# Two packed attentions of a four-layer model: each round cut into two halves of two heads, with the plain score products issued inside the halves

## The chip, the cores and the metric

The kernel runs on one core of one Trainium2 chip. The time is the device time of the whole kernel in microseconds (us), the median of a few executions; lower is better. Engines are called by their short names: PE is TensorE (matrix products, results in PSUM banks), DVE is VectorE, ACT is ScalarE, POOL is GpSimd, SP issues the loads.

## What is computed

The reference is four layers on `x` (2 batches, 256 tokens, width 128), each an attention (mostly over a context of 512 keys) and a feed-forward part, added to `x`:

```python
x = x + _L1_xattn_ref(_layernorm(x), ctx_1024, ctx_1024, mask_SxS2_bk0, Wq, Wk, Wv, Wo)   # 16 heads of 8, 512 keys, masked
x = x + _L1_ffn_ref(_layernorm(x), ...)   # begins with self-attention: 16 heads of 8, 256 keys; then a mixture of experts
```

The change touches only these two attentions, called L1x and L1f below. Both have 16 heads of width 8: scores = q·k, softmax over the keys, times the values.

## The kernel before

**Packing.** A head of width 8 would use 8 of PE's 128 rows. Four heads (a "head group", `HG = 4`, `NG = 4` groups) are laid on the four quarters of 32 rows: head j of a group on rows 32j to 32j+31. A product on one quarter and products on other quarters can run side by side in PE. Queries and keys are held in three 8-row parts (high and low halves of a 16-bit split), so a quarter has 24 used rows.

**Iterations and rounds.** An iteration `it` is one head group and one batch (8 in all). A round `r` takes 256 keys of an iteration: L1x has 512 keys, so `rpi = 2` rounds per iteration and 16 rounds; L1f has 256 keys, `rpi = 1`, 8 rounds.

**What a round does.** The softmax needs the row maximum before the exponential. The scores are therefore computed twice:

1. `natural(nr, part)` (L676), the plain products: queries on the output's rows, one product of 512 columns per head and query tile (L1x), or two of 256 (L1f). Four of them, numbered `w`, belong to a round, two in each `part`; head quarter j is `w % 4`. They go to a ring of three PSUM banks (S0, S1, M; `ring`, L637), and DVE takes the maximum of each (`stat`, L1830 in L1x with the mask, L1824 in L1f), which empties the bank.
2. `spread(it)` writes the maxima of an iteration into a matrix `m16`, by three small operations: on DVE for the first two iterations (L1836 to L1838), on POOL after that (L2453 or L2456, L2459, L2462).
3. `turn_max(it)` (L691) turns `m16` on PE into a ring bank, and DVE's `with_max` (L1846) adds it to the queries.
4. `scores(r)` (L713): keys on the output's rows, maxima included: 8 products of 256 columns, four heads times two key tiles (`cc`), into two pairs of PSUM banks, one pair for heads 0 and 1, one for heads 2 and 3. Ahead of them, in all 128 rows, four products of 512 columns bring in the mask (L702, L1x) or two are there to keep PE busy (L705, L1f).
5. ACT takes the exponential of each pair of banks (L1409, two per round).
6. `values(r-1)` (L727): 8 products of 32-bit data, each as two instructions, in quarters of columns, into bank O.

Every fourth round (L1x) or second round (L1f) ACT copies bank O out (L1434), PE turns it (`turn_out`, L736) and DVE divides by the sums (`norm`, L1854 to L1857). For the next head group PE repeats the queries (`RQ`, L661), and in L1f the keys (`RK`, L637), in a ring bank, and ACT copies them out.

**Order on PE.** The order is written by hand in `pe_packed`. The plain products run `lead = rpi + 1` rounds ahead. An iteration of the loop is: `scores(r)`, `natural(r+lead, 0)`, `values(r-1)`, `turn_max` when an iteration of heads begins next, `RQ`/`RK`, `turn_out`, `natural(r+lead, 1)`. Where no plain products are left, spare products (L381) stand in their place; some also stand in the head (L684, two after each part).

**Order on DVE.** `stat` 0 and 1, `with_max`, `norm`, `stat` 2 and 3, then `spread` for the first two iterations.

**POOL.** Before it spreads maxima, POOL splits seven blocks of values for layer 2 into halves (`FILL`; L2550 the high half, L2553 the rest). While it waits for maxima later, it splits layer 2's weights and context (L2515, L2517).

Of the kernel before, what the change touches and what calls it, by code (L numbers as in the profile page):

```python
# [25 lines left out]
P = 128  # L26
B, S, D = 2, 256, 128
# [59 lines left out]


# [5 lines left out]
DVE_SPREADS = 2  # L94
L1X = Packed("L1x", SK, mask=True)
# [30 lines left out]
def build(nc, A, out):  # L126
    with ExitStack() as ctx:
# [527 lines left out]
        def pe_packed(pe, a, last_v):  # L655
# [8 lines left out]
            def natural(nr, part):  # L664
# [6 lines left out]
                for w in range(4 * s + 2 * part, 4 * s + 2 * part + 2):  # L671
# [22 lines left out]
            def scores(r):  # L694
                it, c = divmod(r, rpi)
                g, b = divmod(it, B)
                for hp in range(2):
                    if r:
                        pe.wait_ge(sem(f"{n}.exp"), 2 * r - 1 + hp)
                    for hh in range(2 if a.mask else 1):  # L700
                        if a.mask:
                            pe.matmul(pairs[hp][:, hh, :], ident16[:],  # L702
                                      maskT[:, 2 * c:2 * c + 2, :].rearrange("p k q -> p (k q)"), start=True, stop=False)
                        else:
                            pe.matmul(pairs[hp][:, hh, :], ident16[:], ident16[:].unsqueeze(1).broadcast_to([P, 4, P]),  # L705
                                      start=True, stop=True)
# [11 lines left out]
            def values(r):  # L718
                it, c = divmod(r, rpi)
                g, b = divmod(it, B)  # L720
                pe.wait_ge(sem(f"{n}.exp"), 2 * r + 2)
                if g and b == 0 and c == 0:
                    pe.wait_ge(sem(f"{n}.out"), g)
                for cc in range(2):
                    kc = 2 * c + cc
                    for j in range(HG):
                        mm = pe.matmul(bank["O"][HR * j:HR * j + VR, b * S:(b + 1) * S], Vaug[:, b * kt + kc, HG * g + j, :],  # L727
                                       PX[(2 * r + j // 2) % 4][:, j % 2, cc * S:(cc + 1) * S],
                                       start=(kc == 0), stop=(kc == kt - 1))
                mm.then_inc(sem(f"{n}.pv"), 1)  # L730
# [20 lines left out]
            for r in range(-a.lead, a.rounds + 2):  # L751
                if r == 0:
                    for b in ("S3", "T0", "T1", "O"):
                        if fills[b]:
                            pe.wait_ge(free[b], fills[b])
                if 0 <= r < a.rounds:
                    scores(r)
                if r + a.lead < a.rounds:
                    natural(r + a.lead, 0)
                if r == 1:  # L760
                    for v in last_v:
                        emptied(pe, v)
                if r + a.lead >= a.rounds and r <= a.rounds:
                    ring_spare(pe, a, 4 if r == a.rounds else 2)
                if 1 <= r <= a.rounds:
                    values(r - 1)
                if (r + 1) % rpi == 0 and 0 <= (r + 1) // rpi < NG * B:
                    turn_max((r + 1) // rpi)
# [14 lines left out]
                if r + a.lead < a.rounds:  # L783
                    natural(r + a.lead, 1)
# [800 lines left out]
        def _(dve):  # L1585
# [228 lines left out]
            def packed(a, last=(), behind=()):  # L1814
                n, rpi, kt = a.name, a.rpi, a.kt

                def stat(nr, k):
                    it, s = divmod(nr, rpi)
                    w = 4 * s + k
                    ps = filled(dve, f"{n}.N{it}.{w}")  # L1820
                    if w == 0 and it >= DVE_SPREADS + 2:
# [5 lines left out]
                    if nr or k >= 2:  # L1827
# [906 lines left out]
```

## Time and profile before

| | |
|---|---|
| median of 3 runs | 543.66 us (543.61 to 546.74) |
| the profiled execution | 545.07 us in all, span 543.4 us from first to last instruction |
| granted PE clock, mean | 0.997 |
| PE busy | 501.9 us (92%), 4897 matmuls |
| DVE busy | 433.2 us (80%) |
| ACT busy | 341.4 us (63%) |
| POOL busy | 277.8 us (51%) |
| L1x | first plain product 172.83 us, end of the last values 237.05 us |
| L1f | first plain product 253.38 us, end of the last values 287.49 us |

The matmuls are pipelined. A record of one lasts longer than its stream of columns, and the next may start under it. So times of PE are read from start to start. A few matmul records are missing from the trace.

### The profile page before, as it was taken

To read this page: it belongs to the slowest core of one execution; us is meant where nothing else is said; L and a number is where in the kernel's file an instruction comes from. 1 tells how busy PE (TensorE), PEld (TensorE's weight loads), DVE (VectorE), ACT (ScalarE), POOL (GpSimd) and SP (SyncE) were. 2 spreads that over 40 slices of the span, in tenths; PEclk is the share of its full clock that TensorE was granted. 3 is DMA by queue.
4 is the path that set the end of the run, shared out by engine and by line. 5 is a ranking of instruction groups with operands and counts; after the bars stand their busy time and mean duration, and the time that the engine had idled before them with its cause. 6 is when DMAs were issued, how large, how long until landed. Compare 5 with 4: busy or idle time off the path is not lost.

```text
span 543.4 us, 13303 instructions
## 1 busy us (share of the span) xinstructions
PE 501.9 (92%) x4897; PEld 290.3 (53%) x4905; DVE 433.2 (80%) x1210; ACT 341.4 (63%) x683; POOL 277.8 (51%) x303
## 2 busy tenths in 40 slices
PE   8889999999999799998998999989999999899996
PEld 4356655667853233343334567635666656864574
DVE  6999999997785788736867899877777788577763
ACT  5698888888246366643762877748878888422212
POOL 7957777777735634400131734038878887300100
PEclk9999999999999899999999999999999999999999
DMA  9660000001130000000002031000000002000000
GB/s 246 125 185 3 1 2 3 1 2 42 39 118 0 2 1 1 3 1 0 2 1 79 22 93 42 2 1 1 2 3 1 2 2 80 2 0 1 2 0 21
DMA packets 24084, 15.43 MB, mean 28 GB/s; under 512 B 8083, under 2 KB 22230, under 8 KB 23894
## 3 DMA queue, kind: packets, MB, share of 16 engines
q1 hardware_dynamic: 24022, 14.60, 9.9%
q8 instruction: 39, 0.64, 0.5%
q14 instruction: 23, 0.19, 0.1%
HBM read 14.33 MB, written 0.26 MB: 27 GB/s over the span
## 4 chain that ended last, share of the span: by engine, by line
PE 52%; DVE 18%; issue 15%; POOL 9%; ACT 6%; DVEq 0%; POOLq 0%; ACTq 0%
PE pspair L513 7%; PE psO L528 4%; PE psS L499 4%; PE psM L471 4%; PE psO L727 3%; PE pspair L702 3%; PE pspair L1004 2%; PE psS L381 2%; DVE nmx L1824 2%; PE pspair L499 2%; POOL PP L2425 2%; ACT PP L1346 2%; DVE Zt L1715 2%; POOL PP L2422 2%; PE psS L676 2%
## 5 line engine op out<-in xcount | busy, mean ns | idle before, releaser
L513 PE MATMUL pspair<-ident,PP 128*128 128x128 f32 x512 | 82.1, 283 | 2.2 <-ACT PP L1346 1.9
L513 PEld LDWEIGHTS pspair<-ident,PP 128*128 128x128 f32 x512 | 54.2, 141 | 30.1 <-issue 20.2
L528 PE MATMUL psO<-V,PP 128*128 128x64 f16 x1536 | 65.7, 193 | 4.2 <-DVE Oall L1756 3.8
L528 PEld LDWEIGHTS psO<-V,PP 128*128 128x128 f16 x1536 | 59.7, 98 | 11.1 <-issue 4.5
L1722 DVE TENSOR_TENSOR PP<-pspair,PP 128x512 f16<-128x512 f32 x66 | 45.4, 688 | 22.8 <-ACT PP L1330 22.6
L1409 ACT ACTIVATE PP<-pspair 128x1024 f32<-128x1024 f32 x48 | 46.5, 1021 | 26.2 <-PE pspair L713 26.1
L2411 POOL TENSOR_TENSOR ln_rs<-ln_ve,minus_half 128x4 f32<-128x4 f32 x10 | 10.3, 1032 | 81.7 <-DVE ln_ve L1612 78.5
L1346 ACT ACTIVATE PP<-scores_m,nm 128x512 f32<-128x512 f32 x64 | 46.5, 726 | 5.4 <-DVE nm L1706 5.4
L2422 POOL TENSOR_TENSOR PP<-acc,one 128x512 f16<-128x512 f32 x32 | 33.3, 1040 | 31.0 <-ACT acc L1328 31.0
L2422 POOL TENSOR_TENSOR PP<-y_sb,one 128x512 f16<-128x512 f32 x30 | 31.2, 1040 | 16.0 <-ACT y_sb L1328 16.0
L1330 ACT CAST PP<-pspair 128x512 f16<-128x512 f32 x66 | 38.3, 581 | 1.1 <-PE pspair L513 1.1
L2425 POOL TENSOR_TENSOR PP<-acc,PP 128x512 f16<-128x512 f32 x32 | 37.1, 1160 | 2.5
L2425 POOL TENSOR_TENSOR PP<-y_sb,PP 128x512 f16<-128x512 f32 x30 | 34.8, 1160 | 2.4
L381 PE MATMUL pspair<-ident 128*128 128x512 f16 x134 | 33.9, 379 | 0.0
L471 PE MATMUL psM<-ctxTm,mask_i 128*128 128x512 f16 x99 | 26.9, 380 | 3.0 <-DVE Qst L1728 3.0
L1328 ACT COPY acc<-pspair 128x512 f32<-128x512 f32 x32 | 18.8, 586 | 11.8 <-PE pspair L513 11.8
L727 PE MATMUL psO<-PP,Oall 128*9 128x256 f32 x384 | 25.2, 380 | 0.0
L1346 ACT ACTIVATE PP<-pspair,nm 128x512 f32<-128x512 f32 x32 | 22.2, 695 | 4.3 <-DVE nm L1700 4.2
L1346 ACT ACTIVATE PP<-psS,nm 128x512 f32<-128x512 f32 x32 | 22.4, 700 | 3.1 <-DVE nm L1700 3.1
L1328 ACT COPY y_sb<-pspair 128x512 f32<-128x512 f32 x30 | 17.6, 587 | 10.4 <-PE pspair L513 10.3
L1700 DVE TENSOR_REDUCE nm<-psS 128x1 f32<-128x512 f32 x32 | 21.5, 675 | 1.1 <-PE psS L499 1.0
L1700 DVE TENSOR_REDUCE nm<-pspair 128x1 f32<-128x512 f32 x32 | 21.9, 683 | 0.2
(596 smaller groups left out, 1261.0 us busy)
## 6 DMA issues: line engine op xcount, KB each, us to landing
W<-in_L_ffn_W SPq DMA_DIRECT2D x16, 256.0 KB, 3.0
bigw<-in_L_xattn_w_q SPq DMA_DIRECT2D x2, 512.0 KB, 6.8
bigw<-in_L_xattn_w_kv SPq DMA_DIRECT2D x1, 1024.0 KB, 4.8
V<-in_ctx SPq DMA_DIRECT2D x1, 512.0 KB, 3.9
bigw<-in_L_xattn_w_v SPq DMA_DIRECT2D x1, 512.0 KB, 5.5
mask_b<-in_mask_BxS_ff SPq DMA_DIRECT2D x1, 512.0 KB, 6.6
bigw<-in_L_xattn_w_k SPq DMA_DIRECT2D x1, 512.0 KB, 5.8
bigw<-in_L_xattn_w_o SPq DMA_DIRECT2D x1, 512.0 KB, 3.9
```

Source lines behind the costliest of these rows:

```text
L381: pe.matmul(bank[b], ident16[:], ident16[:].unsqueeze(1).broadcast_to([P, 4, P]), start=True, stop=True)
L471: mm = pe.matmul(bank["M"][:], (wq16 if what == "Q" else wk16)[:, wpart, cols_], X16[:, cpart, :] if what == "Q" else ctxTm16[:, cpart, keys],
L513: mm = pe.transpose(bank[f"T{j % 2}"][:, k * P:(k + 1) * P], Pb[j % 4][:, k * P:(k + 1) * P], ident[:])
L528: mm = pe.matmul(bank["O"][:, (j % UPH) * a.dv:(j % UPH + 1) * a.dv], (PTH, PTL)[ppart][j % 4][:, k * P:(k + 1) * P], (VH, VL)[vpart][:, b ...
L727: mm = pe.matmul(bank["O"][HR * j:HR * j + VR, b * S:(b + 1) * S], Vaug[:, b * kt + kc, HG * g + j, :], PX[(2 * r + j // 2) % 4][:, j % 2, ...
L1330: nc.scalar.copy(PTH[j % 4][:, 0:a.keys], ps[:, 0:a.keys]).then_inc(sem(f"{n}.high"), 1)
L1346: nc.scalar.activation(Pb[j % 4][:, 0:a.keys], src[:, 0:a.keys], ACT.Exp, bias=nm[:, j % 4:j % 4 + 1], scale=-1.0 if a.mask else 1.0, accu ...
L1409: nc.scalar.activation(PX[k % 4], pairs[k % 2][:], ACT.Exp, scale=a.scale).then_inc(sem(f"{n}.exp"), 1)
L1700: dve.tensor_reduce(nmc, ps[:, 0:a.keys], AX.X, ALU.max, negate=True)\
L1722: dve.tensor_tensor(PTL[j % 4][:, 0:a.keys], ps[:, 0:a.keys], PTH[j % 4][:, 0:a.keys], ALU.subtract).then_inc(free[f"T{j % 2}"], 1)
L2422: pool.tensor_tensor(PTH[j % 4], P32[j // 2 % 2], one[:].broadcast_to([P, SK]), ALU.mult)\
L2425: pool.tensor_tensor(PTL[j % 4], P32[j // 2 % 2], PTH[j % 4], ALU.subtract)\
```

## The change

`HALVES = ((2, 3), (0, 1))` gives the heads whose plain products go with each half. The changes, part by part:

- `scores(r, hp, between)` now does one half, the pair of heads `2*hp, 2*hp+1`: its mask or busy products, the two products of key tile 0, then the plain products `natural(between, hp)` of the two other quarters, then the two products of key tile 1.
- `values(r, cc)` does one key tile.
- The order on PE in the middle rounds is scores half 0, values of key tile 0 of the round before, scores half 1, `turn_max`, values of key tile 1, then `RQ`/`RK` and `turn_out`.
- In the head (`r < 0`) the second part of the last round of plain products comes behind the first half of round 0, and the first `turn_max` ahead of it; the spare products behind it go.
- On DVE `with_max` comes behind the first maximum (r < 1) or behind the third, and `norm` behind all four.
- The iteration's last maximum is now head 1's (`last_max`).
- POOL waits for the first spread (`L1x.m16`) between the two halves of its fourth value block (k = 3).

```diff
@@ natural
-                for w in range(4 * s + 2 * part, 4 * s + 2 * part + 2):
+                for w in (4 * s + HALVES[part][0], 4 * s + HALVES[part][1]):
...
-                elif nr < a.lead:
+                elif nr < a.lead - part:
                     for _ in range(2):
                         pe.matmul(pairs[0][:, 0, :], ident16[:], ...)
@@ scores
-            def scores(r):
+            def scores(r, hp, between=None):
...
-                for hp in range(2):
-                    if r:
-                        pe.wait_ge(sem(f"{n}.exp"), 2 * r - 1 + hp)
-                    for hh in range(2 if a.mask else 1):
...
+                if r:
+                    pe.wait_ge(sem(f"{n}.exp"), 2 * r - 1 + hp)
+                else:
+                    for bk in ("S2", "S3") if hp == 0 else ("T0", "T1"):
+                        if fills[bk]:
+                            pe.wait_ge(free[bk], fills[bk])
+                for hh in range(2 if a.mask else 1):
...
-                if c == 0:
+                if c == 0 and hp == 0:
                     emptied(pe, f"{n}.mT{it}")
                 for cc in range(2):
-                    for j in range(HG):
+                    if cc == 1 and between is not None and between < a.rounds:
+                        natural(between, hp)
+                    for j in (2 * hp, 2 * hp + 1):
@@ values
-            def values(r):
+            def values(r, cc):
...
+                if cc == 0:
+                    pe.wait_ge(sem(f"{n}.exp"), 2 * r + 2)
+                    if r == 0 and fills["O"]:
+                        pe.wait_ge(free["O"], fills["O"])
+                    if g and b == 0 and c == 0:
+                        pe.wait_ge(sem(f"{n}.out"), g)
@@ the loop of PE
+                nr, turned = r + a.lead, (r + 1) // rpi if (r + 1) % rpi == 0 else NG * B
+                if r < 0:
+                    natural(nr, 0)
+                    if r < -1:
+                        natural(nr, 1)
+                    else:
+                        turn_max(0)
+                elif r == 0:
+                    scores(0, 0)
+                    natural(nr - 1, 1)
+                    scores(0, 1)
+                    natural(nr, 0)
+                    if turned < NG * B:
+                        turn_max(turned)
+                    natural(nr, 1)
+                elif r < a.rounds:
+                    scores(r, 0, nr)
...
+                    if nr >= a.rounds:
+                        ring_spare(pe, a, 2)
+                    values(r - 1, 0)
+                    scores(r, 1, nr)
+                    if turned < NG * B:
+                        turn_max(turned)
+                    values(r - 1, 1)
+                elif r == a.rounds:
+                    ring_spare(pe, a, 4)
+                    values(r - 1, 0)
+                    values(r - 1, 1)
@@ the loop of DVE
+                    before_max = 1 if r < 1 else 3
                     if nr < a.rounds:
-                        stat(nr, 0)
-                        stat(nr, 1)
+                        for i in range(before_max):
+                            stat(nr, i)
                     if (r + 1) % rpi == 0 and 0 <= (r + 1) // rpi < NG * B:
                         with_max((r + 1) // rpi)
+                    if nr < a.rounds:
+                        for i in range(before_max, 4):
+                            stat(nr, i)
+                        if (nr + 1) % rpi == 0 and nr // rpi < DVE_SPREADS:
+                            spread(nr // rpi)
...
-                    if nr < a.rounds:
-                        stat(nr, 2)
-                        stat(nr, 3)
-                        if (nr + 1) % rpi == 0 and nr // rpi < DVE_SPREADS:
-                            spread(nr // rpi)
@@ POOL, the value blocks
                 pool.wait_ge(sem("L2.vhigh"), k + 1)
+                if k == 3:
+                    pool.wait_ge(sem("L1x.m16"), 1)
                 pool.tensor_tensor(VL[:, n // 2, half], ...)
```

## Rows read from the trace of the kernel before

**Rows 1.** The page: granted PE clock in 40 equal slices of the span.
```profile
PEclk9999999999999899999999999999999999999999
```

**Rows 2.** Chain of waits of 191 to 223 us (rounds of L1x), by line.
```profile
by line: PE psO L727 30.7%; PE pspair L702 30.1%; PE psS L676 11.9%; PE pspair L713 10.3%; PE psM L676 6.1%; issue 3.0%; PE psS L736 2.8%; PE psS L691 2.0%; PE psM L691 1.4%; PE psS L661 1.4%; PE psM L661 1.4%
```

**Rows 3.** Windows (head, clock drop, rounds 2-11, rounds 12-15, L1f): us, busy per engine, PEclk.
```profile
172.83:190.79 17.96, 15.16 (x78) 4.34 (x79) 14.58 (x45) 6.70 (x9) 12.77 (x12) 0.90 0.01 1
181.99:185.41 3.42, 3.20 (x11) 0.93 (x16) 1.37 (x5) 0.53 (x1) 3.26 (x4) 0.50 0.00 0
190.79:222.92 32.13, 31.33 (x338) 11.12 (x343) 28.07 (x92) 21.29 (x24) 12.99 (x25) 1.00 0.00 1
222.92:237.05 14.13, 13.92 (x148) 4.67 (x150) 6.67 (x28) 8.26 (x10) 3.92 (x6) 1.00 0.01 2
262.94:283.33 20.39, 18.78 (x226) 7.50 (x226) 16.16 (x34) 15.04 (x18) 5.00 (x19) 1.00 0.01 2
```

**Rows 4.** Timeline of PE, rounds 4 and 5 of L1x: start us, us, what.
```profile
197.47 0.81 PE L702 MATMUL pspair<-Amat,ident 128*128 128x512 bf16 x3 [0.16 <-issue]
198.22 0.40 PE L713 MATMUL pspair<-Ast,scores_m 26*128 26x256 f16 x8
198.44 0.38 PE L676 MATMUL psS<-scores_m,Qst 24*128 24x512 f16 x2
198.75 1.05 PE L727 MATMUL psO<-PP,Oall 128*9 128x256 f32 x16
199.74 0.38 PE L676 MATMUL psM<-scores_m,Qst 24*128 24x512 f16 x1
...
200.06 1.19 PE L702 MATMUL pspair<-Amat,ident 128*128 128x512 bf16 x4
201.18 0.40 PE L713 MATMUL pspair<-Ast,scores_m 26*128 26x256 f16 x8
...
202.70 0.28 PE L691 MATMUL psS<-ident,Amat 128*128 128x128 f16 x2
```

**Rows 5.** Timeline of ACT in the same rounds.
```profile
198.65 1.94 ACT L1409 ACTIVATE PP<-pspair 128x1024 f32<-128x1024 f32 x2 [1.07 <-PE pspair L713]
200.47 0.59 ACT L1434 COPY tmp<-psO 128x512 f32<-128x512 f32 x1
```

**Rows 6.** Timeline of PE, one round of L1f.
```profile
266.43 0.27 PE L676 MATMUL psM<-Oall,Qst 24*128 24x256 f16 x1
266.49 0.28 PE L676 MATMUL psS<-Oall,Qst 24*128 24x256 f16 x1
266.54 0.27 PE L676 MATMUL psM<-Oall,Qst 24*128 24x256 f16 x1
...
268.12 0.27 PE L691 MATMUL psS<-ident,Amat 128*128 128x128 f16 x2 [0.26 <-POOL Amat L2462]
```

**Rows 7.** Timeline of DVE, the same round of L1f.
```profile
264.99 0.29 DVE L1846 TENSOR_TENSOR Ast<-psS,Qst 128x256 f16<-128x256 f16 x1
265.75 1.29 DVE L1824 TENSOR_REDUCE nmx<-psS 128x2 f32<-128x512 f32 x2 [0.46 <-PE psS L676]
```

**Rows 8.** Timeline of POOL: head of L1x, and a spread of L1f.
```profile
183.81 1.04 POOL L2550 TENSOR_TENSOR V<-mask_b,one 128x512 f16<-128x512 f32 x1
...
267.12 0.25 POOL L2453 TENSOR_SCALAR mq<-nmx 128x8 f32<-128x8 f32 x1 [2.58 <-DVE nmx L1824]
```

**Rows 9.** Timeline of DVE, head of L1x: the first spread, and the second.
```profile
178.53 0.85 DVE L1836 TENSOR_SCALAR mq<-nmx 128x8 f32<-128x8 f32 x1
179.41 0.98 DVE L1837 CAST Amat<-mq 128x8 f16<-128x8 f32 x1
...
188.55 0.17 DVE L1836 TENSOR_SCALAR mq<-nmx 128x8 f32<-128x8 f32 x1
```

**Rows 10.** Timeline of PE, head of L1x, the first turn; and the scores of round 2.
```profile
180.76 0.27 PE L691 MATMUL psS<-ident,Amat 128*128 128x128 f16 x2 [1.38 <-DVE Amat L1838]
...
191.75 0.40 PE L713 MATMUL pspair<-Ast,scores_m 26*128 26x256 f16 x8
```

More of the change, by code:

```diff
@@ L86, in __init__, with last_max @@
         self.lead = self.rpi + 1
+    def last_max(self, it):
+        return f"{self.name}.N{it}.{4 * (self.rpi - 1) + HALVES[1][1]}"
 HG = 4
@@ L94 @@
 DVE_SPREADS = 2
+HALVES = ((2, 3), (0, 1))
 L1X = Packed("L1x", SK, mask=True)
@@ L716, in scores @@
                             mm.then_inc(sem(f"{n}.st"), 1)
-            def values(r):
+            def values(r, cc):
                 it, c = divmod(r, rpi)
                 g, b = divmod(it, B)
[L721 to L730, printed above, removed]
+                if cc == 0:
[4 more added lines that the diff above has]
+                        pe.wait_ge(sem(f"{n}.out"), g)
+                kc = 2 * c + cc
+                for j in range(HG):
+                    mm = pe.matmul(bank["O"][HR * j:HR * j + VR, b * S:(b + 1) * S], Vaug[:, b * kt + kc, HG * g + j, :],
+                                   PX[(2 * r + j // 2) % 4][:, j % 2, cc * S:(cc + 1) * S],
+                                   start=(kc == 0), stop=(kc == kt - 1))
+                if cc == 1:
+                    mm.then_inc(sem(f"{n}.pv"), 1)
             def turn_out(g):
@@ L751, in pe_packed @@
             for r in range(-a.lead, a.rounds + 2):
[L752 to L768, printed above, removed]
+                nr, turned = r + a.lead, (r + 1) // rpi if (r + 1) % rpi == 0 else NG * B
[3 more added lines that the diff above has]
+                        natural(nr, 1)
+                    else:
+                        turn_max(0)
[9 more added lines that the diff above has]
+                    scores(r, 0, nr)
+                    if r == 1:
+                        for v in last_v:
+                            emptied(pe, v)
+                    if nr >= a.rounds:
[9 more added lines that the diff above has]
+                    values(r - 1, 1)
                 g, q = divmod(r + a.lead + 2, B * rpi)
@@ L1815, in packed, with stat @@
                 n, rpi, kt = a.name, a.rpi, a.kt
-                def stat(nr, k):
+                heads_in_turn = HALVES[0] + HALVES[1]
+                def stat(nr, i):
                     it, s = divmod(nr, rpi)
-                    w = 4 * s + k
+                    w = 4 * s + heads_in_turn[i]
                     ps = filled(dve, f"{n}.N{it}.{w}")
-                    if w == 0 and it >= DVE_SPREADS + 2:
+                    if s == 0 and i == 0 and it >= DVE_SPREADS + 2:
                         dve.wait_ge(sem(f"{n}.m16"), it - 1)
@@ L1826, in stat @@
                         return
[L1827 to L1829 removed]
+                    if nr or i >= 2:
+                        it2, s2 = divmod(nr if i >= 2 else nr - 1, rpi)
+                        emptied(dve, f"{n}.N{it2}.{4 * s2 + heads_in_turn[(i - 2) % 4]}")
                     dve.tensor_tensor_reduce(P32[w % 2], ps[:], mask_n[:, w // HG, :], -1.0, 60000.0 * MSCALE, ALU.add,
```

19 lines of the change are left out of this document (7 added, 12 removed).

## The prediction, made before the changed kernel was run

> **What bounds the kernel now.** I read the page first: PE is busy for 92% of the span and its granted clock is full in all slices but one [rows 1]. The change touches only L1x and L1f, about 64 and 34 us of 543. So I asked of each stretch which wait ends last. In the middle rounds of L1x the chain of waits is PE's own work: values, mask products, plain products and scores, and only 3.0% "issue" [rows 2]; PE is busy 31.33 of 32.13 us, DVE 28.07, ACT 21.29 [rows 3]. In L1f no engine fills the time: PE 18.78 of 20.39 us, DVE 16.16, ACT 15.04 [rows 3]. There a turn waits for POOL's spread [rows 6], which waits for DVE's last maximum [rows 8]. The head of L1x is the third place: 17.96 us at a mean clock of 0.90, with 3.42 us of it at 0.50, the lower level of 1.2 GHz [rows 3], behind an idle stretch of PE of 1.38 us in which the first turn waits for DVE's spread [rows 10].
>
> **PE's prices, start to start [rows 4].** Products of 512 columns follow each other at (0.81 - 0.38)/2 = 0.216 us. The last of the mask products at 197.47 starts at 197.90, the scores at 198.22: 0.216 and 0.10 for the switch from all rows to quarters. Scores (8 of 256 columns, four side by side) take 198.44 - 198.22 = 0.23. Plain products, two side by side: to the values 198.75 - 198.44 = 0.31, so 0.216 and 0.09 for the switch. Values: 1.05 - 0.38 = 0.67 over three steps is 0.22 for each four of the 16, so 0.87 of the 0.99 to the next plain products, and 0.12 for the switch. Plain products to mask products 0.32, again 0.10. A switch costs 0.09 to 0.12.
>
> **A middle round of L1x, before and after.** Before (rounds 4, 5): mask 0.87, switch 0.10, scores 0.23, plain 0.216, switch 0.09, values 0.87, switch 0.12, plain 0.216, switch 0.10: 2.81. After, each half: mask 0.44, switch 0.10, a stretch in quarters in which two quarters take 256 and 256 columns and the other two 512, so 0.23 if they run side by side, switch 0.09, values 0.44, switch 0.12: 1.41, the round 2.82. The second pass of plain products is hidden (0.43 gone), but the four-quarter scores now take two stretches (0.23 more) and there are two more switches (0.20). Net nothing. What goes is the wait for the exponential: the mask products of 200.06 take 1.12 to the scores at 201.18 [rows 4] where 0.87 + 0.10 is due, so 0.15 in two rounds.
>
> Bounds for the new stretch in quarters: 0.23 if all quarters stream on their own, 0.11 more if the second key tile waits for the plain products. I take 0.23, by this row: the third plain product in program order starts at 266.49, in its own quarter, before the second at 266.54 [rows 6]. The Trainium skill says otherwise on its page "TensorE: Matmul & The Clock Gate" (Part 3, The mechanism): matmuls keep program order in start and end. By that rule each of L1f's ten stretches with plain products (two of 256 columns on each quarter, one behind the other) would take 0.33, 1.0 us more in all; the row disagrees, and L1x, with one product per quarter, would not change.
>
> **New waits in the middle.** ACT starts an exponential 0.20 after the scores' stream ends (198.65 against 198.22 + 0.23) [rows 4, 5]; one takes 1.02 (1.94 for two) [rows 5]. From the second half's scores to the values of the next round PE now has 0.09 + 0.44 + 0.12 + 0.54 + 0.23 + 0.09 = 1.51 of work, and needs 0.20 + 1.02 + 0.05 = 1.27: no wait. But in the rounds with an out copy (0.59, [rows 5]) ACT ends at 1.27 + 0.59 = 1.86, and the first values after it overwrite bank O: 0.35 wait, three times in L1x. The ring has three banks; a maximum takes 0.61 (1.29 - 0.68 for the second of two, [rows 7]), a pair every 1.41: DVE keeps up, except where no `RQ` or `turn_out` stretches a pair (once, 0.3). Rounds 2 to 11: five times -0.15, + 3 x 0.35 (one of them outside), + 0.3: from 32.13 to 32.2, **+0.1**.
>
> **Tail of L1x.** From round 13 on there are no plain products to hide. Before, spare products stood once per round. After, the round has them once too, plus the second stretch in quarters 0.23 and the two switches, with nothing saved: +0.5 for each of rounds 13 to 15, less the exponential's wait: **+1.45** on the 14.13 us of that window [rows 3]. The same in L1f for rounds 6 and 7 (one busy product per half there): **+0.75**.
>
> **Head of L1x.** The spread cost 0.85 and 0.98 for two operations that take 0.17 and as little in the next iteration [rows 9] (0.62 for all three, gaps included); POOL was splitting value blocks then. POOL's new wait clears it: m16 at 178.53 + 0.62 = 179.15 and not 180.61, the turn follows at 179.3, PE has hardly a gap and the clock stays full. `with_max` comes behind one maximum and not two: 179.15 + 0.61 + 0.29 = 180.05. The scores of round 0 start at 181 (behind `RQ`, 0.44, and the mask products) and not 185.3. From there DVE sets the time: six maxima (0.61 each; the first waits for a plain product of about 181.1, which is there at 181.5) end at 185.2, the second spread 0.62, three maxima 1.84 and `with_max` 0.29 give 187.95, the scores of round 2 at 188.4. But POOL, held back by 1.05 us, now splits its last block from 184.9 (183.81 + 1.05, [rows 8]) to 187.1, across the second spread. Bounds for that spread: 0.62 clear of POOL, or 2.1 as the first one was. I take 1.7: the first operation waits for the one in flight (0.75), and a later one may lose again. Scores of round 2 at 189.5, before 191.75 [rows 10]: **-2.2** (-3.3 to -1.8; with the clock down again as before, another +1.7, since 3.20 us of PE work at 0.50 [rows 3] would take 1.6).
>
> **Head and rounds of L1f.** The second spread ends some 0.3 later than before, because two of its maxima wait until the first half of round 0 is done (scores 0.23, then 0.42 until the product is there, where before they stood ahead of the round). PE idles some 1.1 us before that turn, and the next two plain products wait for banks that DVE frees only behind the spread and `with_max`. One wait more for a maximum behind `with_max` (0.61) and the spread's 0.3, less the 0.26 by which the half mask of round 0 is shorter: the scores of round 1 come at 263.6, not at 262.94, where the last window of [rows 3] begins: **+0.65**. Then a round: PE 2 x (0.22 + 0.10 + 0.23 + 0.09 + 0.44 + 0.12) = 2.4, turn 0.22 (two products of 128 columns and a switch), repeats 0.44 (two of 512): 3.05, and 3.3 on average with `turn_out` (0.44 every second round); DVE 4 x 0.61 + 0.29 [rows 7] = 2.73, and 3.1 with `norm`. The old loop (maximum, POOL's spread from 267.12 on [rows 8] to the turn at 268.12 [rows 6], plain products, maximum) took 20.39 for the six rounds of the last window of [rows 3], 3.4 each; it falls off the path, since the plain products no longer stand behind the turn. So 0.1 to 0.3 per round is won, but in round 3 the values wait for the out copy, which stands on ACT behind the third `RQ` copy, now issued last in PE's round: 0.8. Six rounds: **0.0**.
>
> **Sum.** -2.2 + 0.1 + 1.45 + 0.65 + 0.75 + 0.0 = +0.75 us. The profiled execution, 545.07, would become 545.8; it lay 1.4 above the median of 543.66. Forecast 544.4 us: no measurable change, the head's gain given back in tails and switches. The out copies, POOL's wait elsewhere and the moved `norm` are otherwise hidden: ACT has 10 us free in rounds 2 to 11 [rows 3], and layer 2's splits are needed 170 us later.
>
> **Rivals.** (A) The added switches cost nothing, because a half as short as this lets the weights of the next kind load early; and the 0.35 waits vanish. 2 x 0.10 x 24 rounds = 4.8 less: 539.6. For it: DVE and POOL have room. Against: none of the switches in [rows 4] is free. (B) Slower: PE's clock falls in one or both heads. Place: L1f before the second turn, and L1x before it, where DVE and POOL hold PE. L1x fell to 0.50 behind a gap of 1.38 [rows 3, 10]; I expect gaps of 1.1 and up to 1.7. Price 1.7 each: 547.8. It decides as soon as a gap with little work around it reaches that of 180.76. (C) The quarters don't run side by side: 0.11 for each of 34 half rounds with plain products, +3.7: 548.1. (D) The change doesn't reach the head: the first spread finds POOL in an operation anyway, since POOL's wait stands behind the high half of a block and that half (1.04, [rows 8]) could slip under the spread; gain lost: 546.6.
>
> **Chances.** Forecast 0.55 (its own range 543 to 546), A 0.17, B 0.15, C 0.07, D 0.06. The range reaches down to A and up to B: 539.8 to 547.8. A measurement of this kernel tells about 1% (5.4 us) from no change. Below 538.2 needs A and a clear head: 0.05. Above 549.1 needs B and C together, or more waits than I see: 0.05. Within 1%: 0.90.
>
> **What would show it.** Head: two short spread operations on DVE, scores of round 2 near 189.5, no slice below 9 in PE's clock at 182. Middle: half rounds of 1.41, plain products recorded inside the scores' stretch of 0.23, waits of PE on the out copy. Tail: from the scores of round 12 to the last values 1.4 us more than before. L1f: scores of round 1 at +0.65 of the stage's start, rounds of 3.1 to 3.3. Wrong if half rounds come out under 1.35 or over 1.5, or if the clock falls.

## The result, and the profile after

| | before | after |
|---|---|---|
| median | 543.97 us (543.6 to 547.38, 6 runs) | 551.05 us (550.4 to 552.32, 6 runs) |
| ratio | | 1.0107, 95% interval 1.0078 to 1.0136 |
| profiled execution | 545.07 us, span 543.4 | 550.40 us, span 548.7 |

The change makes the kernel 1.1% slower; the forecast was 544.4 us, the range ended at 547.8. Executions of one kernel differ by some us, and the longer ones mostly show a lower mean granted clock; where in the kernel the clock fell is known for the profiled execution alone. So the account below goes stage by stage in the profiled executions, and a drop is named wherever it falls.

The page after, granted PE clock in 40 slices: the weak slice has moved from the 14th (177 to 190 us, L1x) [rows 1] to the 20th (261 to 274 us, L1f).

```profile
PEclk9999999999999999999799999999999999999999
```

Windows of after, columns as in [rows 3]: L1x's head, rounds 2 to 11, rounds 12 to 15; L1f's head, rounds 1 to 5, rounds 6 and 7; and the stretch of the clock drop. (A stage begins with the first scores of its first round; the expectations below call the window of L1f's rounds 1 to 5 "rounds 1 to 6", from the scores of the one to those of the other.)

```profile
172.65:189.59 16.94, 14.38 (x80) 4.08 (x81) 15.32 (x48) 6.90 (x9) 12.74 (x12) 1.00 0.00 1
189.59:222.15 32.56, 31.46 (x341) 8.92 (x345) 28.27 (x92) 22.43 (x24) 13.77 (x25) 1.00 0.00 1
222.15:237.36 15.21, 15.16 (x146) 4.29 (x146) 5.78 (x26) 8.57 (x9) 3.17 (x6) 1.00 0.01 2
253.85:264.82 10.97, 9.29 (x52) 2.91 (x52) 8.91 (x20) 3.42 (x5) 0.44 (x2) 0.87 0.00 0
264.82:284.73 19.91, 18.23 (x195) 5.48 (x194) 14.40 (x29) 13.44 (x16) 3.06 (x14) 0.90 0.01 2
284.73:292.82 8.09, 8.09 (x82) 2.67 (x81) 2.45 (x9) 4.48 (x5) 4.99 (x7) 1.00 0.01 2
...
262.02:268.85 6.83, 6.55 (x43) 1.42 (x44) 4.72 (x10) 2.63 (x3) 0.71 (x3) 0.50 0.01 2
```

The same three windows of L1f, before:

```profile
253.38:262.94 9.56, 8.37 (x56) 2.64 (x57) 8.29 (x20) 3.69 (x5) 0.00 (x0) 1.00 0.00 0
262.94:280.35 17.41, 16.19 (x195) 6.68 (x194) 14.63 (x32) 12.62 (x15) 3.50 (x15) 1.00 0.01 2
280.35:287.49 7.14, 6.75 (x81) 2.50 (x80) 3.04 (x9) 4.36 (x5) 4.98 (x7) 1.00 0.01 2
```

L1x takes 64.7 us and not 64.1: its head won 2.0 (it was 18.9), the rounds lost 0.4, the tail lost 2.2. L1f takes 39.0 and not 34.1: +1.4, +2.5, +0.9. The stretches before, between and behind the two attentions are the same to 0.2 us. So between these two executions nearly the whole difference is L1f's, and 6.83 us of L1f run at a granted clock of 0.50, the level of 1.2 GHz, which before did not happen there. L1x looks nearly even only because the profiled execution before spent 3.42 us of its head at 0.50 [rows 3] and the one after did not; e1 prices such a drop at 1.5 us. At equal clock L1x lost about 2.1 us.

**Head of L1x.** Timeline of DVE after, the two spreads; then POOL at the second one, and PE's longest wait there.

```profile
178.34 0.17 DVE L1863 TENSOR_SCALAR mq<-nmx 128x8 f32<-128x8 f32 x1
178.55 0.18 DVE L1864 CAST Amat<-mq 128x8 f16<-128x8 f32 x1
178.77 0.19 DVE L1865 TENSOR_TENSOR Amat<-mq,Amat 128x8 f16<-128x8 f32 x1
...
185.05 0.71 DVE L1863 TENSOR_SCALAR mq<-nmx 128x8 f32<-128x8 f32 x1
185.79 0.18 DVE L1864 CAST Amat<-mq 128x8 f16<-128x8 f32 x1
186.01 1.01 DVE L1865 TENSOR_TENSOR Amat<-mq,Amat 128x8 f16<-128x8 f32 x1
```
```profile
184.69 1.04 POOL L2578 TENSOR_TENSOR V<-mask_b,one 128x512 f16<-128x512 f32 x1
185.80 1.16 POOL L2583 TENSOR_TENSOR V<-mask_b,V 128x512 f16<-128x512 f32 x1
```
```profile
187.66 0.39 PE L681 MATMUL psS<-scores_m,Qst 24*128 24x512 f16 x1 [1.41 <-DVE nmx L1857]
```

The first spread is short, as foreseen. The second meets POOL's last block: its first operation ends at 185.76, POOL's at 185.73; its third at 187.02, POOL's at 186.96. Each lasts until POOL's instruction ends. DVE's next maximum comes late by it, and PE waits 1.41 us for the ring bank which that maximum empties. The instruction that waits is a plain product issued in round 1, not the turn (that starts at 188.28): since the change it stands between the two key tiles of the scores, and the rest of the round is held up behind it. The Trainium skill, page "SBUF — State Buffer", section "SBUF: two separate sides", calls the port pair that DVE and POOL share an exclusive lock held for the whole instruction; these ends agree.

**Middle of L1x.** Timeline of PE after: half a round, and a wait.

```profile
191.10 0.28 PE L723 MATMUL pspair<-Ast,scores_m 26*128 26x256 f16 x2
191.11 0.39 PE L681 MATMUL psS<-scores_m,Qst 24*128 24x512 f16 x1
191.11 0.39 PE L681 MATMUL psM<-scores_m,Qst 24*128 24x512 f16 x1
191.22 0.27 PE L723 MATMUL pspair<-Ast,scores_m 26*128 26x256 f16 x2
191.43 0.62 PE L739 MATMUL psO<-PP,Oall 128*9 128x256 f32 x8
191.98 0.39 PE L710 MATMUL pspair<-Amat,ident 128*128 128x512 bf16 x1
...
199.65 0.62 PE L739 MATMUL psO<-PP,Oall 128*9 128x256 f32 x8 [0.34 <-ACT tmp L1459]
```

The plain products stream beside both key tiles of scores: 0.33 from the first scores to the values, 0.55 from there to the mask products. Where nothing waits the half round is 1.41 (191.10 to 192.51), as worked out, and the 0.35 wait for the out copy is there (0.34 at 199.65).

**L1f.** Timeline of PE after, each row with a wait; then ACT at the last of them.

```profile
261.61 0.27 PE L696 MATMUL psS<-ident,Amat 128*128 128x128 f16 x2 [0.95 <-DVE Amat L1865]
...
270.20 0.26 PE L681 MATMUL psM<-Oall,Qst 24*128 24x256 f16 x1 [0.39 <-ACT Oall L657]
...
274.58 0.62 PE L739 MATMUL psO<-PP,Oall 128*9 128x256 f32 x8 [0.70 <-ACT tmp L1459]
```
```profile
273.37 0.58 ACT L1310 CAST Qst<-psS 128x512 f16<-128x512 f32 x1 [0.42 <-PE psS L666]
273.85 0.59 ACT L1459 COPY tmp<-psO 128x512 f32<-128x512 f32 x1
```

PE idles 0.95 us before the second turn, and the clock is down from 262.02 to 268.85. Then it waits 0.39 for a ring bank that the copy of `RK` frees, and 0.70 for the out copy, which stands behind the copy of `RQ`.

### The profile page after: what moved, and what is told of

Its sections match the earlier page's. It is cut to its first block, busy times and chain, and to the rows that moved or that the text cites. A ratio compares the mean times of both kernels' runs of the same rounds, so it can differ in the third digit from the quotient of the medians.

```text
span 548.7 us, 13297 instructions
## 1 busy us (share of the span) xinstructions
PE 506.3 (92%) x4893; PEld 285.8 (52%) x4901; DVE 433.1 (79%) x1210; ACT 343.5 (63%) x683; POOL 277.8 (51%) x303
## 4 chain that ended last, share of the span: by engine, by line
PE 50%; DVE 20%; issue 15%; POOL 8%; ACT 6%; DVEq 0%; POOLq 0%; ACTq 0%
PE pspair L518 6%; PE psO L739 4%; PE psO L533 4%; PE psS L504 4%; PE psM L476 4%; PE pspair L1029 2%; PE pspair L710 2%; PE pspair L723 2%; DVE V L1680 2%; PE pspair L504 2%; POOL PP L2453 2%; DVE nmx L1851 2%; ACT PP L1371 2%; DVE Zt L1740 2%; POOL PP L2450 2%
## 5 line engine op out<-in xcount | busy, mean ns | idle before, releaser
L533 PE MATMUL psO<-V,PP 128*128 128x64 f16 x1536 | 65.7, 193 | 4.3 <-DVE Oall L1781 3.8
L1434 ACT ACTIVATE PP<-pspair 128x1024 f32<-128x1024 f32 x48 | 49.1, 1024 | 26.4 <-PE pspair L723 26.3
L2439 POOL TENSOR_TENSOR ln_rs<-ln_ve,minus_half 128x4 f32<-128x4 f32 x10 | 10.3, 1032 | 85.9 <-DVE ln_ve L1637 82.8
L2450 POOL TENSOR_TENSOR PP<-acc,one 128x512 f16<-128x512 f32 x32 | 33.3, 1040 | 31.2 <-ACT acc L1353 31.1
L2453 POOL TENSOR_TENSOR PP<-y_sb,PP 128x512 f16<-128x512 f32 x30 | 34.8, 1161 | 2.4
L739 PE MATMUL psO<-PP,Oall 128*9 128x256 f32 x384 | 30.2, 391 | 1.4 <-ACT tmp L1459 1.4
L1353 ACT COPY y_sb<-pspair 128x512 f32<-128x512 f32 x30 | 17.6, 587 | 10.5 <-PE pspair L518 10.4
```

Of the source, the lines that this page charges most:

```text
L533: mm = pe.matmul(bank["O"][:, (j % UPH) * a.dv:(j % UPH + 1) * a.dv], (PTH, PTL)[ppart][j % 4][:, k * P:(k + 1) * P], (VH, VL)[vpart][:, b ...
L1353: nc.scalar.copy(P32[j // 2 % 2], ps[:]).then_inc(free[f"T{j % 2}"], 1)
L1434: nc.scalar.activation(PX[k % 4], pairs[k % 2][:], ACT.Exp, scale=a.scale).then_inc(sem(f"{n}.exp"), 1)
L2450: pool.tensor_tensor(PTH[j % 4], P32[j // 2 % 2], one[:].broadcast_to([P, SK]), ALU.mult)\
L2453: pool.tensor_tensor(PTL[j % 4], P32[j // 2 % 2], PTH[j % 4], ALU.subtract)\
```

## The experiments

In e1, e2, e6, e7 and e12 each attention has three switches: the heads of the halves, `new_head` (order of the rounds up to 0), and `first_old`, the first round from which on PE and DVE use the whole order of the kernel before. A table of the stages stands at the end of the section. Each ratio is to executions of the kernel before taken beside it (medians 545.02 us for e1 to e4, 544.85 for e5 to e8, 545.18 for e9 to e12). One execution of each kernel was profiled; the stages, and the place of a clock drop, are those of that one.

**e1: L1f as before, L1x and POOL as changed.**

```diff
+L1F.halves, L1F.new_head, L1F.first_old = ((0, 1), (2, 3)), False, 1
```

> The changed kernel with L1f in its old order (head, rounds, tail and the order of DVE), L1x new. Stage L1f is read from its first plain product to the end of its last values: 34.1 us before, 39.0 changed. Theory 1 (the loss is L1f's): L1f 34.1, total 4.8 us below the changed kernel, some 546 us, 0.5 above before, and the clock full throughout L1f. Rival 2 (the loss lies outside the two attentions, in phases that the change only shifts): total stays at 549 to 551.

Measured: 548.20 us (10 runs), ratio 1.0046 (1.0027 to 1.0065); L1f 34.13, at full clock: in the profiled execution the loss of L1f is gone. The total is not the 0.5 above before that was expected, but 2.5 by the ratio: so the change of L1x costs too. L1x took 66.19, with the clock down from 190.06 to 193.47, just behind the gap of 1.41 (here its rounds 2 to 11 take 34.05 and not 32.56, so a drop of 3.41 us costs 1.5). None of the ten executions ran at full clock; the mean clock was 0.990 to 0.997.

**e2: L1x as before (and no wait on POOL), L1f as changed.**

```diff
+L1X.halves, L1X.new_head, L1X.first_old = ((0, 1), (2, 3)), False, 1
-                if k == 3:
-                    pool.wait_ge(sem("L1x.m16"), 1)
```

> The kernel before with L1f alone in the new order; L1x old, without POOL's new wait. Theory 1 (the loss is L1f's): L1f 39.0 us, total +4.8 against before, some 548.8. If the clock fell in L1f only because of what L1x left behind (rival 3: the clock's state is carried over, not made in L1f), L1f comes out at 35 to 36 us and the clock stays full there.

Measured: 550.13 us (6 runs), ratio 1.0068 (1.0038 to 1.0099). L1f 38.87, its clock at 0.50 from 262.92 for 6.83 us: the drop comes with L1f's new order whether L1x is new (after) or old (here, where L1x had a drop of 10.2 us of its own), so it is not carried over from the new L1x.

**e3: five spare products before L1f's second turn.** (In L1x no turn follows round 0, so the line issues none there.)

```diff
                     if turned < NG * B:
+                        spare(pe, "O", 5)
                         turn_max(turned)
```

> The changed kernel with five spare products of 512 columns (5 x 0.216 = 1.08 us) in the gap of 0.96 us ahead of L1f's second turn. Theory 1a (the gap lets the granted clock fall to 0.50 for 6.8 us, and that is what L1f lost): clock full, L1f 39.0 - 3.2 = about 35.8, total 3 us below the changed kernel. Rival 1b (the order with its waits on ring banks and the out copy costs the 4.8, the low clock runs under it): clock full, L1f still above 38.

Measured: 549.67 us (548.25 to 551.74, 9 runs), ratio 1.0071 (1.0042 to 1.0099). Windows of L1f, same three as above:

```profile
253.91:264.07 10.16, 9.25 (x57) 3.29 (x56) 8.79 (x20) 3.21 (x5) 0.00 (x0) 1.00 0.00 0
264.07:282.58 18.51, 16.76 (x195) 5.50 (x194) 14.47 (x30) 13.65 (x16) 3.50 (x15) 1.00 0.01 2
282.58:290.66 8.08, 8.08 (x82) 2.67 (x81) 2.44 (x9) 4.48 (x5) 4.98 (x7) 1.00 0.01 2
```

In the profiled execution the clock stays full and L1f gives back 38.97 - 36.75 = 2.2 us, less than the theory's 3.2; it does not stay above 38 as the rival had it. The other 2.6 of its loss are not the clock: head +0.60, rounds +1.1, tail +0.93.

**e4: the kernel before with POOL's wait alone.**

```diff
                 pool.wait_ge(sem("L2.vhigh"), k + 1)
+                if k == 3:
+                    pool.wait_ge(sem("L1x.m16"), 1)
```

> The kernel before with POOL's new wait alone (POOL waits for the first spread between the halves of its fourth value block). Theory 1 (the head's gain is the cleared spread and the clock that stays full): the first two spread operations take 0.17 and 0.19 instead of 0.85 and 0.98, the clock stays full at 182 us, the scores of round 2 come 1.5 to 2.5 us earlier, total 541.5 to 542.5. Rival: the second spread meets POOL's held-back blocks and takes it all back, total 543.5 to 544.5.

Measured: 543.09 us (10 runs), ratio 0.9963 (0.9943 to 0.9984). The median is above the 541.5 to 542.5 of the theory. L1x's head takes 16.94 us, the same as with the whole change: the wait is the head's gain, and the new order adds nothing to it. Of that gain of 2.0 us about 1.5 is the clock: those executions of the kernel before that ran at a mean clock of 0.998 or more took 543.44 to 543.90 us, only some 0.4 above e4's.

Beside the time of the stage the new order takes something away. Here the second spread meets POOL too (1.02 us for its last operation), but PE's longest wait behind it is 0.46 us, before the turn, and 9 of the 10 executions have a mean clock of 0.998 or more. e1 differs from this run in L1x's order alone, has the wait of 1.41, and has none of 10.

**e5: e3 with the out copy first on ACT.**

```diff
+                g, q = divmod(r, B * rpi)
+                if q == 0 and 1 <= g <= NG:
+                    act.wait_ge(sem(f"{n}.pv"), r)
...
+                    nc.scalar.copy(Osb, bank["O"][:]).then_inc(sem(f"{n}.out"), 1)
                 g, q = divmod(r + a.lead + 2, B * rpi)
...
                             repeated_k(g, c)
-                g, q = divmod(r, B * rpi)
...
-                    nc.scalar.copy(Osb, bank["O"][:]).then_inc(sem(f"{n}.out"), 1)
```

> The changed kernel with the five spare products of e3 before the second turn, and on ACT the copy of bank O placed ahead of the copies of RQ and RK instead of behind them. Theory: the wait of 0.7 us before the values of round 3 of L1f is the out copy standing behind the RQ copy of 0.59; it falls to about 0.1, rounds 1 to 6 of L1f go from 18.51 to 17.9 us, the span from 546.5 to about 545.9. Rival: what is late then is the ring bank that the RQ copy frees 0.59 later, so the wait moves to the plain products and L1f stays at 36.75.

Measured: 549.56 us (4 runs), ratio 1.0094 (1.0074 to 1.0114), with the clock in L1x's head down for 6.83 us in the profiled run. In L1f ACT now copies bank O first:

```profile
272.52 0.58 ACT L1453 COPY tmp<-psO 128x512 f32<-128x512 f32 x1
273.02 0.58 ACT L1311 CAST Qst<-psS 128x512 f16<-128x512 f32 x1
```

PE's wait is gone (values at 273.47, 0.34 behind the scores) and rounds 1 to 5 take 17.73 instead of 18.51. The theory held for L1f: 0.8 us of the 1.1 was this order. The total does not show it, since the clock fell in L1x.

**e6: e3 with the tails whole.**

```diff
+L1X.first_old, L1F.first_old = 13, 6
```

> The changed kernel with the five spare products of e3, but the rounds that have no plain products left (L1x from round 13, L1f from round 6) in the old whole order. Theory: the tails lose 2.2 and 0.93 us by the split alone (two more switches and one more stretch in quarters per round, two exponentials that no longer overlap the same work): L1x from the scores of round 12 comes back from 15.22 to about 13.1, L1f's tail from 8.08 to about 7.2, span 543.4 to 543.6. Rival: only the switches come back (0.2 per round, 5 rounds: 1.0 us), because the exponentials of the last halved round are late anyway: span 545.5.

Measured: 547.60 us (4 runs), ratio 1.0064 (1.0043 to 1.0085). L1x's tail takes 13.87, neither the theory's number (13.1) nor the rival's (only the switches back, 0.2 per round). The last rounds show why. PE, last round of L1x (round 15) from its first scores, after and then before:

```profile
232.69 0.39 PE L723 MATMUL pspair<-Ast,scores_m 26*128 26x256 f16 x4
233.01 0.60 PE L386 MATMUL psS<-ident 128*128 128x512 f16 x2
233.54 0.62 PE L739 MATMUL psO<-PP,Oall 128*9 128x256 f32 x8
234.10 0.60 PE L710 MATMUL pspair<-Amat,ident 128*128 128x512 bf16 x2
234.63 0.39 PE L723 MATMUL pspair<-Ast,scores_m 26*128 26x256 f16 x4
234.96 0.62 PE L739 MATMUL psO<-PP,Oall 128*9 128x256 f32 x8
235.51 1.04 PE L386 MATMUL psS<-ident 128*128 128x512 f16 x4
```
```profile
233.19 0.40 PE L713 MATMUL pspair<-Ast,scores_m 26*128 26x256 f16 x8
233.51 0.61 PE L381 MATMUL psS<-ident 128*128 128x512 f16 x2
234.05 1.05 PE L727 MATMUL psO<-PP,Oall 128*9 128x256 f32 x16
235.03 1.04 PE L381 MATMUL psS<-ident 128*128 128x512 f16 x4
```

From the first scores to the last spares it is 2.82 after and 1.84 before. Of the 0.98, 0.53 are the second half's mask products (234.10 to 234.63): before, all mask products of a round lie ahead of its first scores, after, half of them lie behind. A boundary "first scores of a round" stands 0.53 earlier in the work after than before. e6 pays that back where it turns from halves to whole rounds (round 12 to 13 takes 3.83 us in e6 and 3.13 in e3), and wins 1.34 of the 2.21. L1f came back by 0.93 in all, from 36.75 to 35.82, as the theory had it.

**e7: the heads of the change alone, with e3's spares.**

```diff
+L1X.first_old, L1F.first_old = 1, 1
```

> The heads of the change alone (order of round 0, DVE's order there, POOL's wait, the spares of e3), all rounds from 1 on in the old whole order. Theory: the halves cost what L1x lost behind its head and most of what L1f lost: L1x 62.1 us (head 16.9, rounds 32.1, tail 13.0, the same as with POOL's wait alone, so the new order of the head gives nothing beyond it), L1f 34.8 (head 10.2, rounds 1 to 6 17.4, tail 7.15); span 542.0. Rival: L1f's rounds are long because the second spread is late and everything behind it runs late: then they stay near 18.5 and the span is 543.1.

Measured: 546.69 us (5 runs), ratio 1.0037 (1.0013 to 1.0060). L1f 34.75 with rounds at 17.2 and a tail of 7.15: the halves cost L1f 36.75 - 34.75 = 2.0, and no delay is carried on from the head. L1x 63.55, with a clock drop from 189.45 to 192.86 (1.5 at e1's price): 62.05 without it, e4's number. But none of the five executions has a mean clock above 0.997, where nine of e4's ten have.

**e8: the kernel before with two waits on POOL.**

```diff
+                if k == 6:
+                    pool.wait_ge(sem("L1x.m16"), 2)
                 pool.tensor_tensor(VH[:, n // 2, half], ...)
...
+                if k == 3:
+                    pool.wait_ge(sem("L1x.m16"), 1)
```

> The kernel before with POOL's wait for the first spread (as e4) and a second one: before its last value block (k = 6) POOL waits for the second spread. Theory: in e4 the second spread still met POOL (0.38 and 1.03 us for operations that take 0.17 and 0.20 in the clear); clear of it, it takes 0.62 and the scores of round 2 come 0.9 us earlier (head 16.0 against 16.94), span 540.6, ratio to the kernel before 0.9945. Rival: behind the spread PE waits only 0.46 us in e4 and DVE's maxima set the time, so 0.4 at most is won: span 541.1, ratio 0.996.

Measured: 542.02 us (541.92 to 542.12, 6 runs), ratio 0.9955 (0.9941 to 0.9968). DVE's second spread, and the window of L1x's head:

```profile
185.38 0.17 DVE L1836 TENSOR_SCALAR mq<-nmx 128x8 f32<-128x8 f32 x1
185.58 0.19 DVE L1837 CAST Amat<-mq 128x8 f16<-128x8 f32 x1
185.80 0.20 DVE L1838 TENSOR_TENSOR Amat<-mq,Amat 128x8 f16<-128x8 f32 x1
```
```profile
172.64:188.58 15.94, 14.74 (x84) 4.38 (x84) 14.08 (x48) 6.69 (x9) 12.81 (x12) 1.00 0.00 2
```

The spread takes 0.62 us (185.38 to 186.00), the head 15.94 and the span is 540.2, as the theory had it or a little better; the ratio's interval holds both its 0.9945 and the rival's 0.996. No kernel here was faster (e9 is its equal): two waits, nothing else. Against the kernel before at full clock (543.50 to 543.76 in the same set) the gain is some 1.6 us, and the rest is that the clock no longer falls: the mean is 0.998 or more in all six.

**e9: e8 with the out copy first on ACT** (the edit of e5 made to e8).

> The kernel before with POOL's two waits (e8) and, on ACT, the copy of bank O ahead of the copies of RQ and RK. Theory: the old order too loses time in round 3 of L1f to the out copy behind the RQ copy (that round takes 4.27 us from scores to scores, its neighbours 3.44 and 2.97); the round falls to about 3.5 as it did from 4.76 to 3.98 in e5, L1f from 34.16 to 33.4, span 539.5, ratio to the kernel before 0.994. Rival: in the old order the plain products that wait for RQ's bank stand between, the wait moves to them, and L1f stays at 34.16, ratio 0.9955.

Measured: 542.09 us (12 runs), ratio 0.9949 (0.9928 to 0.9970), L1f 34.16 as in e8. Nothing was won, but not for the rival's reason: no wait stood there at all. The copy now ran from 265.27 to 265.86 and the values it is for started at 267.06, right behind scores and plain products; the long round is nearly all PE's own work (turn, `RK`, `turn_out`), with the turn's 0.26 wait for POOL. The wait of e5 is one that the change made.

**e10: the change with all repairs.** It is e5 with POOL's second wait:

```diff
+                if k == 6:
+                    pool.wait_ge(sem("L1x.m16"), 2)
```

> The changed kernel with everything found so far repaired: spares before L1f's second turn, the out copy first on ACT, and POOL's second wait before its last value block. Theory: the second spread is clear of POOL, the gap of 1.41 us before the second turn in L1x shrinks to about 0.5, so PE's clock falls in neither head in any run; L1x head 16.0, rounds 2 to 12 32.6, tail 15.2; L1f 36.0; span 545.0, clock 1.0, ratio 1.002 to 1.005: the halves stay a loss against the kernel before and some 4.8 us against e8. Rival (the halves themselves are neutral and the loss was clock and collisions): span 541 or less.

Measured: 546.62 us (546.1 to 550.2, 12 runs), ratio 1.0026 (1.0001 to 1.0051). Windows: L1x's head, all of L1x, all of L1f:

```profile
172.92:188.54 15.62, 14.37 (x77) 4.07 (x80) 14.00 (x48) 6.91 (x9) 12.79 (x12) 1.00 0.01 2
172.92:236.32 63.40, 61.01 (x559) 17.28 (x566) 48.05 (x163) 37.90 (x42) 29.73 (x42) 1.00 0.01 2
252.81:288.78 35.97, 34.02 (x332) 11.41 (x331) 25.62 (x57) 21.37 (x25) 8.48 (x22) 1.00 0.01 2
```

Against e8 (61.06 and 34.16) the halves with the new heads still cost 2.3 and 1.8 us. That the clock would fall in no run was wrong: 6 of the 12 show a mean clock of 0.993 to 0.997, and these are the six slowest (546.80 to 550.20).

**e11: two spares instead of five.**

```diff
-                        spare(pe, "O", 5)
+                        spare(pe, "O", 2)
```

> The changed kernel with two spare products before L1f's second turn, not five: of PE's gap of 0.955 us there about 0.5 is left. Theory: the length of the gap with little work around it decides; with 0.5 (the kernel before has 0.42 there and keeps its clock) L1f keeps full speed, head 10.2, rounds 18.5, L1f 36.7, as with five. Rival: what decides is the head's thin work as a whole (the waits behind the turn too), then the clock falls again at about 262 for 3.4 or 6.8 us and L1f takes 38 to 39.

Measured: 552.39 us (4 runs), ratio 1.0119 (1.0075 to 1.0162). PE's waits in L1f's head were 0.42 and 0.41 us, no longer than before the change, and the clock fell all the same, later:

```profile
257.10:294.95 37.85, 34.81 (x329) 11.05 (x328) 25.66 (x57) 21.34 (x25) 8.49 (x22) 0.95 0.01 2
266.94:270.36 3.42, 3.42 (x29) 0.63 (x27) 1.86 (x4) 1.75 (x3) 0.70 (x3) 0.50 0.02 5
185.03:195.26 10.23, 9.75 (x64) 1.62 (x63) 7.40 (x23) 3.88 (x4) 2.56 (x3) 0.50 0.01 2
```

The theory that the length of one gap decides fell; the rival, the thin head as a whole, has this run for it, though it was not tested by itself. What exactly decides stays open: the same L1x head ran at full clock in the profiled run of e3 and at 0.50 for 3.4, 6.8 and 10.2 us in those of e1, e5 and e11.

**e12: L1f's head in the old order, its rounds in halves, no spares.**

```diff
+L1F.new_head = False
```

> The changed kernel with the head of L1f (rounds up to 0) in the old order on PE and DVE and its rounds from 1 on in halves, no spares. Theory: the clock falls in L1f because of the new order of the head alone; here it stays, the head takes 9.6 us, rounds 1 to 6 18.5, the tail 8.1: L1f 36.2, span 546.0 (or 1.5 more if the clock falls in L1x's head). Rival: the halved rounds 1 and 2 with their waits for ring banks are thin enough themselves; then the clock falls all the same and L1f takes 38 or more.

Measured: 549.33 us (8 runs), ratio 1.0076 (1.0049 to 1.0104):

```profile
255.48:291.76 36.28, 33.22 (x329) 10.79 (x328) 25.61 (x57) 21.36 (x25) 8.51 (x22) 1.00 0.01 2
```

The clock stays full in L1f. This is one execution; the seven others have mean clocks of 0.987 to 0.997, and where it fell in them is not known. But the fourteen profiled executions agree: it fell in L1f in the three with the new head and fewer than five spares (after, e2, e11) and in none of the other eleven. Without that head L1f is 36.28, so the halves alone cost 2.1 and the new head 0.5 (36.75 - 36.28) beside the clock.

The stages of the profiled executions, us, from starts in the timelines ("down": how long the clock was at 0.50 there):

| | head | r 2-11 | tail | L1x | down | head | r 1-5 | tail | L1f | down | span |
|---|---|---|---|---|---|---|---|---|---|---|---|
| before | 18.9 | 32.1 | 13.0 | 64.1 | 3.4 | 9.6 | 17.4 | 7.1 | 34.1 | 0 | 543.4 |
| after | 16.9 | 32.6 | 15.2 | 64.7 | 0 | 11.0 | 19.9 | 8.1 | 39.0 | 6.8 | 548.7 |
| e1 | 16.9 | 34.1 | 15.2 | 66.2 | 3.4 | 9.6 | 17.4 | 7.1 | 34.1 | 0 | 545.4 |
| e2 | 20.5 | 32.1 | 13.0 | 65.7 | 10.2 | 11.0 | 19.8 | 8.1 | 38.9 | 6.8 | 549.8 |
| e3 | 16.9 | 32.6 | 15.2 | 64.7 | 0 | 10.2 | 18.5 | 8.1 | 36.8 | 0 | 546.5 |
| e4 | 16.9 | 32.1 | 13.0 | 62.1 | 0 | 9.6 | 17.4 | 7.1 | 34.1 | 0 | 541.5 |
| e5 | 17.9 | 33.1 | 15.2 | 66.3 | 6.8 | 10.2 | 17.7 | 8.1 | 36.0 | 0 | 547.5 |
| e6 | 16.9 | 34.0 | 13.9 | 64.9 | 3.4 | 10.2 | 18.7 | 6.9 | 35.8 | 0 | 545.9 |
| e7 | 17.3 | 33.3 | 13.0 | 63.6 | 3.4 | 10.4 | 17.2 | 7.1 | 34.8 | 0 | 543.6 |
| e8 | 15.9 | 32.1 | 13.0 | 61.1 | 0 | 9.6 | 17.5 | 7.1 | 34.2 | 0 | 540.2 |
| e9 | 15.9 | 32.1 | 13.0 | 61.1 | 0 | 9.6 | 17.5 | 7.1 | 34.2 | 0 | 540.2 |
| e10 | 15.6 | 32.6 | 15.2 | 63.4 | 0 | 10.2 | 17.7 | 8.1 | 36.0 | 0 | 544.6 |
| e11 | 17.9 | 34.2 | 15.2 | 67.3 | 10.2 | 10.3 | 19.4 | 8.1 | 37.9 | 3.4 | 550.8 |
| e12 | 16.9 | 34.0 | 15.2 | 66.2 | 3.4 | 9.3 | 18.9 | 8.1 | 36.3 | 0 | 547.6 |

Executions with a mean clock of 0.998 or more: 17 of 65 for the kernel before in the three sets, 9 of 10 in e4, 6 of 6 in e8, 9 of 12 in e9, 6 of 12 in e10, none of 6 in e2. Where L1x has the new head and POOL its first wait alone, it is 2 of 40 in the kernels whose L1f kept its clock when profiled (e1, e3, e5, e6, e7, e12), and none of 10 in after and e11, where the drop in L1f would be enough for that.

## Why the prediction was wrong

The sum said +0.75, the profiled executions say +5.3. By its steps:

- **Middle of L1x**, +0.1, measured +0.4. The terms as they stand (five times -0.15, two waits of 0.35 inside the window, 0.3) give +0.25 and not +0.1. The half round was right. A round with an out copy takes 4.03 us from first scores to first scores and one with `RQ` 3.57, where before both took 3.50. The 0.46 between them (rounds 5 and 7) is the out copy, 0.41 more from the scores to the values, and 0.10 from the last values to the next scores, where `turn_out` (1.66) takes longer than `RQ` (1.56), less 0.05 elsewhere.
- **Tail of L1x**, +1.45, measured +2.2. Mis-sized mostly by the boundary: I took the gain of the head up to "the first scores of round 2" and the loss of the tail from the first scores of round 12, and did not see that the change moves half of a round's mask products (0.53) from one side of that mark to the other (e6). And the 0.3 of a late ring bank, which the prediction put into rounds 2 to 11, falls into round 12, whose first half takes 1.71 (222.15 to 223.86). The switches and the extra stretch were put a little high, at 0.5 per round where their own terms give 0.43: round 14 to 15 takes 3.36 and not 2.97, 0.39 more.
- **Head of L1x**, -2.2, measured -2.0 at that mark; as that mark stands 0.53 of PE's work earlier, some -1.5 by the work done (worked out, not measured). The two short operations, the collision of the second spread (1.7 foreseen, 1.97 measured from 185.05 to 187.02) and the scores of round 2 were as described, but the gain was not the new order's: POOL's wait alone makes it all, most of it by the clock (e4). And PE's gap of 1.41 stood before a plain product, a ring bank that the prediction did not list.
- **L1f's head**, +0.65, measured +0.6 at full clock (e3), and its **tail**, +0.75, measured +0.93.
- **L1f's rounds**, 0.0, measured +1.1 at full clock. The out copy's wait was foreseen (0.8; 0.70 measured, 0.78 by e5). Its terms, six rounds at 0.1 to 0.3 won and 0.8 lost, give -1.0 to +0.2, and round 6 is counted in the tail as well. What failed is the side "0.1 to 0.3 per round is won": without repeats rounds 4 and 5 take 3.02 and 3.48 against 2.97 and 3.49, nothing. And the plain products, now inside the scores, wait 0.39 for the bank that `RK` has just taken.
- **The clock**, the step that failed most. The forecast let it be full in L1f; rival B named the place and the gap (1.1, measured 0.95), but at 0.15 and 1.7 us. It fell there in after and e2 for 6.83 us and cost 2.2; twice as long as the row that the price came from [rows 3]. The +5.3 is then 2.2 of L1f's clock, 2.6 of L1f's work, 0.6 of L1x and -0.2 ahead of them. L1x's 0.6 is about 2.1 of work less 1.5 of clock, since the execution before had its drop there and the one after had none. That L1x's clock stayed full, as forecast, was partly the luck of that execution: e1 and e3 have the same L1x, and 2 of their 19 executions ran at full clock.

Rival A fell (no switch was free), rival D fell (the first spread was clear). Rival C fell too: in the half round above the last scores start 0.11 behind the first, beside the plain products. The Trainium skill, page "TensorE: Matmul & The Clock Gate", Part 3, The mechanism, has matmuls keep program order in start and end; the stretch in L1x, 0.33 with its switch, is what quarters side by side give, and the wait-free stretch in L1f (scores at 275.46, turn at 275.79) is also 0.33, not the 0.42 of that rule (the prediction's 0.33 and a switch). Here the trace does not agree with the page.

What the halves and the new heads were worth at best is e10 against e8, which share their waits on POOL and ran at full clock when profiled: a loss of 2.3 us in L1x and 1.8 in L1f. Two halves need every switch twice, and the score products of two quarters cover only half the array; only plain products pay for that, and in 5 of 24 rounds there are none.

## What to carry to other kernels

Take a change apart before judging it: here the only part that paid was one wait on POOL, and alone, with a second like it, it gives the fastest kernel. Ask of a gain how much of it is the clock, and compare executions at the same clock: a drop in the one profiled execution before hid 1.5 us of loss in L1x. When a step is cut in halves, price each seam in both directions, ask what fills the idle quarters in the rounds that have nothing to interleave, and measure stages between marks that the change does not move. In this kernel the drops started in the two heads, where PE waits on small operations of another engine; give the cover work back that a reordering takes out (the change removed L1f's spares there), or clear the engine that makes it wait.

## What was not expected

- Reordering L1f's head took the clock down for 6.83 us (after, e2), while gaps of 0.8 to 1.1 us elsewhere in the same executions (PE idles 1.07 us at about 320 us) passed at full clock. e11 had gaps of only 0.42 and still lost 3.42 us to it.
- The same L1x head with a gap of 1.4 us can run at full clock (after, e3) or spend 3.4 us at the lower level (e1, e6, e12), which costs 1.5. Within one kernel, executions differ by this as much as the change is worth.
- Three operations on 128x8 elements take 0.62 us on DVE in the clear and 1.97 beside POOL's 128x512 ones. Clearing POOL once gave 2.0 us of head (e4), a second time 1.0 (e8). The rearrangement of 24 rounds gave nothing. Of e4's 2.0, about 1.5 is the clock that stayed full.
